# A two-layer transformer on one core: the batch-1 projection becomes steps of the attention program

## The reference

```python
x = layernorm(x + L0_attn(x))   # 16 heads of 16, causal softmax
x = layernorm(x + L0_ffn(x))    # silu(x Wu') * (x Wg') Wd', weights ternary
x = layernorm(x + L1_attn(x))   # 16 query heads, 4 key/value heads, ALiBi,
                                # a window and the global columns masked out
x = layernorm(x + L1_ffn(x))    # silu gate, width 1024

def ternary_quant(w):
    scale = mean(|w|) + 1e-8
    return clip(round(w / scale), -1, 1) * scale
# layer 1 only: queries come from x * sigmoid(sum |x|), keys and values from x
```

## Time and the profile before

| | |
|---|---|
| median of 3 runs | 1161.24 us |
| profiled execution, its own time | 1158.14 us |
| its span | 1156.4 us |
| layer 0: projection, from first transposes to last part | 6.9 to 73.7 us |
| layer 0: opening maxima | 74.6 to 101.0 us |
| layer 0: first exponential's scores | 104.8 us |
| layer 1: projection | 495.1 to 539.2 us |
| layer 1: opening maxima on DVE | 553.4 to 589.5 us |
| layer 1: first exponential's scores | 593.2 us |
| mean granted clock of PE, share of full speed | 0.939 |

### The profile page before, as it was taken

One profiled execution on the slowest core, in us unless ns is written; L12 is line 12 of the kernel. 1 busy time (PEld: TensorE's weight loads), 2 busy tenths in 40 slices (PEclk: granted clock), 3 DMA queues, 4 the chain that ended last, 5 costly groups with the idle time before them and its releaser, 6 DMA issues. The chain is left out here.

```text
span 1156.4 us, 17918 instructions
## 1 busy us (share of the span) xinstructions
PE 1022.1 (88%) x6546; PEld 516.8 (45%) x6546; DVE 725.0 (63%) x1563; ACT 591.5 (51%) x1169; POOL 324.2 (28%) x391
## 2 busy tenths in 40 slices
PE   7947899999988899765779899999999999899996
PEld 4511233333324788642122334334343334588885
DVE  3767877777744655464878677777778744234322
ACT  3412666666675433234026577776777776523220
POOL 1041111111112343302225614224152341324331
PEclk9955999999999999978569899999999999999998
DMA  8585044443000000007932416143260000000001
GB/s 276 127 155 70 1 56 56 56 56 50 7 2 1 2 1 1 1 19 163 235 103 73 103 16 118 36 82 90 29 118 4 32 2 1 1 1 19 19 1 37
DMA packets 32980, 64.20 MB, mean 56 GB/s; under 512 B 6079, under 2 KB 22351, under 8 KB 30516
## 3 DMA queue, kind: packets, MB, share of 16 engines
q1 hardware_dynamic: 31004, 58.07, 25.3%
q0 software_dynamic: 1072, 3.80, 0.9%
q10 hardware_dynamic: 816, 1.18, 0.3%
HBM read 50.45 MB, written 12.32 MB: 54 GB/s over the span
## 5 line engine op out<-in xcount | busy, mean ns | idle before, releaser
L812 ACT ACTIVATE prob<-ps 128x512 f32<-128x512 f32 (+6 forms) x896 | 442.9, 537 | 293.9 <-PE ps L848 286.2
L848 PE MATMUL ps<-qop,kop 98*128 98x512 bf16 (+15 forms) x1376 | 303.5, 292 | 21.1 <-ACT prob L812 8.0
L834 PE MATMUL ps<-kop,qop 96*128 96x512 bf16 (+3 forms) x896 | 273.7, 381 | 53.0 <-DVE maxes L753 24.4
L848 PEld LDWEIGHTS ps<-qop,kop 107*128 107x128 bf16 (+2 forms) x1376 | 114.6, 98 | 280.1 <-ACT prob L812 201.1
L875 PE MATMUL ps<-prob,vst 128*32 128x512 f32 (+4 forms) x1792 | 212.3, 546 | 6.8 <-POOL prob L702 4.7
L753 DVE CUSTOM_DVE_ANT_0 attn<-ps,alibi_table 128x960 bf16<-128x960 f32 x128 | 148.1, 1157 | 87.8 <-PE ps L834 59.0
L702 POOL TENSOR_TENSOR prob<-prob,keep 128x384 int32<-128x384 int32 (+2 forms) x144 | 122.3, 852 | 268.7 <-ACT prob L812 266.5
L1229 PE MATMUL ps<-xs,ffn_parts 128*128 128x512 f32 x640 | 150.4, 392 | 4.5 <-DVE hf L1203 2.3
L753 DVE CUSTOM_DVE_ANT_0 tri<-ps,alibi_table 128x960 bf16<-128x960 f32 x128 | 147.6, 1153 | 3.5 <-PE ps L834 3.5
L834 PEld LDWEIGHTS ps<-kop,qop 96*128 96x128 bf16 x896 | 77.7, 100 | 143.6 <-DVE maxes L753 84.1
L1229 PEld LDWEIGHTS ps<-xs,ffn_parts 128*128 128x128 f32 x640 | 119.0, 188 | 29.7 <-DVE hf L1203 3.1
(11 more groups left out here) (97 smaller groups left out, 710.0 us busy)
## 6 DMA issues: line engine op xcount, KB each, us to landing
alibi_table<-in_table SPq DMA_DIRECT2D x32, 464.0 KB, 5.7
qop<-q_parts SPq DMA_DIRECT2D x96, 128.0 KB, 7.1
kop<-k_parts SPq DMA_DIRECT2D x48, 128.0 KB, 7.7
kop<-k_parts SPq DMA_DIRECT2D x48, 96.0 KB
q_parts<-qop SPq DMA_DIRECT2D x8, 384.0 KB, 3.0
q_parts<-kop SPq DMA_DIRECT2D x8, 384.0 KB, 6.5
x<-in_x SPq DMA_DIRECT2D x4, 512.0 KB, 7.3
out<-x SPq DMA_DIRECT2D x4, 512.0 KB, 2.9
```

The lines of the kernel that those rows point to most:

```text
L812: nc.scalar.activation(prob[0:rows, q % 2, k % HG, lo % CH:lo % CH + hi - lo], ps[0:rows, t_bank(n, k), lo % CH:lo % CH + hi - lo], ACT.Ex ...
L834: last = nc.tensor.matmul(ps[:, S_BANK + 2 * (k % S_SLOTS) + a // CH, a % CH:a % CH + b - a], qop[0:RD, par, h, i0:i0 + P], kop[0:RD, par, ...
L848: return nc.tensor.matmul(ps[0:rows, bank, a % CH:a % CH + b - a], lhs, rhs, start=start, stop=True, skip_group_check=True)
```

## The change

The program `project` is gone; a class `Projection` gives its work as steps of the attention program, so there is one barrier less in each layer.

- The opening is now: all steps of batch 0, then the 32 maxima of group 0 with the steps of batch 1 spread among the first 30 of them, in layer 0 then the three sums of absolutes and the thresholds.
- Turns, units and value items share three PSUM banks (4, 5, 6) in place of six; banks 0 to 3 serve the maxima.
- In batch 0 the copies of turns are shared by ACT and DVE; in batch 1 ACT makes them all, and POOL makes the third parts.
- Layer 0's units run in the order q, k of the first two groups (four units), then of the other two. After four units are stored, SP loads group 0.
- The operand rows are interleaved: product row r of feature d is partition 6d + r instead of 16r + d, so each transfer writes every sixth partition.
- Layer 1 weighs, exponentiates and scales x chunk by chunk instead of all at once, with two chunk buffers.
- The sums of absolute weights move to ACT (one activation with an accumulator for each of three tensors, 128x2048). The ternary weights move to POOL, as twelve steps in groups 1 to 3 of layer 0, each of two comparisons and one subtraction over 128x512. The raw weights are loaded after group 0's operands.
- Layer 1's six table loads are issued first. POOL adds the bias behind the opening instead of beside it.

```diff
+        if layer.index == 0 and 1 <= group <= 3 and selected(layer, half, kt) is None:
+            steps.append(("ternary", 4 * (group - 1) + kt, 0))
...
+def opening_of(layer, proj):
...
+    first = proj.steps(0)
+    behind = proj.steps(1) + [("flush", 0)]
+    maxima = [("max", u, 1) for u in range(len(units_of(layer)))]
+    end = []
+    if layer.index == 0:
+        behind += [("abs", j) for j in range(3)]
+        end = [("total", 0, 0), ("threshold", 0, 0)]
+    out = [(what, k, 0) for what, k in first]
+    for n, unit in enumerate(maxima):
+        out.append(unit)
+        upto = [-(-len(behind) * m // (len(maxima) - 2)) for m in (n, n + 1)]
+        out += [(what, k, 0) for what, k in behind[upto[0]:upto[1]]]
+    return out + end + [("parts", 0, 1), ("rows", 0, 1)]
...
+    BANKS, SIDE = (4, 5, 6), 7
...
+            self.units = [(b, m, c) for b in range(B) for p in range(KD) for c in range(2) for m in (p, KD + p)]
...
+    def steps(self, b):
+
+        half, turned = len(self.units) // 2, len(self.turns) // 2
+        units = [("unit", u) for u in range(b * half, (b + 1) * half)]
+        turns = [("turn", n) for n in range(b * turned, (b + 1) * turned)]
+        if self.i == 0:
+            vs = [("v", v) for v in range(b * 4, b * 4 + 4)]
+            first = [o for j in range(4) for o in (*units[2 * j:2 * j + 2], vs[j])]
+            return turns + first
+        if b == 1:
+            return turns + units + [("v", 1)]
+        out = []
+        for c in range(2):
+            out += [("weigh", c), *turns[4 * c:4 * c + 2], ("divide", c), ("scale", c), *turns[4 * c + 2:4 * c + 4]]
+        out += [*units[:3], ("weigh", 2), *units[3:5], ("weigh", 3), units[5], ("v", 0)]
+        return out + [(what, c) for c in (2, 3) for what in ("divide", "scale")]
...
+    def third_part_behind(self, pool, u):
...
+        self.nc.gpsimd.tensor_tensor(self.part[u % RING][0:r, 2, :], self.rest[0:r, u % RING, :],
+                                     self.part[u % RING][0:r, 1, :], ALU.subtract).then_inc(self.part3[1], 1)
...
+            nc.scalar.activation(self.below, self.raw[k], ACT.Abs, accum_out=self.wsum[:, k:k + 1]
+                                 ).then_inc(self.abs_sum, 1)
...
+            j, cols = k // 4, slice(k % 4 * CH, (k % 4 + 1) * CH)
+            pool.wait_ge(self.tern, 3 + 3 * k)
+            for which, side in enumerate((self.above, self.below)):
+                nc.gpsimd.tensor_scalar(side[:, cols], self.raw[j][:, cols], self.thr[:, which, j:j + 1], 0.0,
+                                        (ALU.is_gt, ALU.is_lt)[which], ALU.add).then_inc(self.tern, 1)
+            pool.wait_ge(self.tern, 5 + 3 * k)
+            nc.gpsimd.tensor_tensor(self.K.wffn[:, j, 0, cols], self.above[:, cols].bitcast(F32),
+                                    self.below[:, cols].bitcast(F32), ALU.subtract).then_inc(self.tern, 1)
...
-            rows = slice(HD * r, HD * (r + 1))
+            rows = slice(r, NPAIR * HD, NPAIR)
...
+            operands.constants(sp, 0)
+            operands.constants(sp, 1)
+
+            for u in range(4):
+                proj.send(sp, u)
+            proj.wait_sent(sp, 4)
+            operands.load(sp, 0)
+            later = len(proj.units) // 2 + 2 + 2 * (1 - i)
+            for u in range(4, later):
+                proj.send(sp, u)
             operands.load(sp, 1)
-            for k in range(RING):
-
-                sp.wait_ge(operands.sent[k], K.parts_in_dram[k])
+            for u in range(later, len(proj.units)):
+                proj.send(sp, u)
+            send_rows(0)
+            proj.wait_sent(sp, len(proj.units))
             operands.constants(sp, BUFS - 1)
             operands.load(sp, BUFS - 1)
```

More of the change, by code:

```diff
@@ L594, in attend @@
         v_heads = HG if i == 0 else 1
+        maxes = sb(st, "maxes" + tag, [P, HG, TB], F32)
+        sums = [sb(st, f"sums{n}" + tag, [P, T], BF16)[:] if n == 0 or i == 0 else K.tri[:] for n in range(2)]
         vst = sb(st, "vst" + tag, [P, BUFS, TB + i, v_heads, 2 * HD], F32)
@@ L605, in attend @@
         rec = sb(st, "rec" + tag, [P, 2, CT * HG], F32)
-        opening = [("max", u, 1) for u in range(NU)] + [("parts", 0, 1), ("rows", 0, 1)]
+        proj = Projection(nc, sem, sb, st, K, L, dram, prep, prob, K.before_weights)
+        opening = opening_of(L, proj)
         def exp_slots(n):
@@ L719, in step @@
                         prep.inverse(pool, k, 0)
+                    elif what in Projection.STEPS:
+                        proj.pool(pool, what, k)
             zero = nc.gpsimd.to_reg(0.0) if i == 0 else None
+            if i == 0:
+                pool.wait_ge(loaded[0], 16 * operands.loads)
+                for j, wt in enumerate(dram.ffn[0]):
+                    wt = wt.rearrange("(k p) n -> p k n", p=P)
+                    pool.dma_start(proj.raw[j].rearrange("p (k n) -> p k n", k=wt.shape[1]), wt
+                                   ).then_inc(proj.ffn_loaded, 16)
+            step(-1, opening)
+            pool.wait_ge(proj.v_done, (8, 1)[i])
             stage(0, 0)
+            pool.wait_ge(proj.xt_full, len(proj.turns))
+            pool.wait_ge(K.tri_loaded, 16 * 5)
             for t in range(NT):
@@ L791, in step @@
                         ).then_inc(normed, 1)
+                    elif what in Projection.STEPS:
+                        proj.dve(dve, what, k)
                     elif what in Preparation.STEPS:
@@ L821, in step @@
                         nc.scalar.copy(ot[:], ps[:, O_BANK, :]).then_inc(evicted, 1)
+                    elif what in Projection.STEPS:
+                        proj.act(act, what, k)
                     elif what in Preparation.STEPS:
                         prep.act(act, what, k)
+            if i == 0:
+                act.dma_start(proj.w[:], dram.wq[0].rearrange("(k p) n -> p k n", p=P)).then_inc(proj.w_loaded, 16)
+            else:
+                act.dma_start(proj.w[:, :, 0:D], dram.wq[1].rearrange("(k p) n -> p k n", p=P)
+                              ).then_inc(proj.w_loaded, 16)
+                act.dma_start(proj.w[:, :, D:proj.width], dram.wkv.rearrange("(k p) n -> p k n", p=P)
+                              ).then_inc(proj.w_loaded, 16)
+            step(-1, opening)
             all_groups(step)
@@ L904, in step @@
                     elif what == "exp":
+                        if n == 0 and k == 0:
+                            proj.wait_all_read(pe)
                         if k == 0:
```

560 lines of the change are left out of this document (285 added, 275 removed).

## The result

The changed kernel takes 1168.65 us (median of 6 runs, 1165.53 to 1172.36) against 1160.77 for the kernel before in the same comparison (6 runs): a ratio of 1.0068, interval 1.0047 to 1.0089. The change made the kernel slower by 0.7%, where 1126 us had been forecast. The profiled execution took 1167.41 us, with a span of 1165.7 and a mean granted clock of 0.942.

What follows compares the result with a forecast made beforehand. Each layer's border was taken as a serial chain: project both batches, load, maxima, exponentials. Gains of 25 us (layer 0) and 10 (layer 1), with 0 behind the borders, took the span from 1156.4 to 1121, median 1126; range 1113 to 1146.

Steps and rivals of the forecast that it cites:

- the ternary step: Layer 0, groups 1 to 3 on GpSimd: 2.3 to 3.9 us a step, four hidden in a 14.99 us gap; taken as 0.
- from 3.7 us a ternary step on, each group's fourth mask is late: Rival, GpSimd late in layer 0's groups: 1141 us at 5 a step, 1174 at 7.7; chance 0.06.
- The residual adds: GpSimd's 10.92 us of adds, now after layer 1's last third part: up to 5 us without the load's cover, taken as 0.
- the third ahead of nothing urgent: Later operand loads on SP (groups 1, 2), issued behind more waits: needed some 30 us later, no cost counted.
- Turns start at 6.9, so units start near 10.6: Start of layer 0: only batch 0's four turns stand ahead of the first unit, which starts near 10.6 us.
- I take issue plus 2 us: 8 us for either layer: First operand load with interleaved rows, each layer: 8 us, bounds 6 (issue alone) and 14.6 (old).
- the load stays slow: Rival: the operand load's shape costs what it cost, both first scores come 6 us later: 1138 us; chance 0.15.
- The tail of layer 0's opening: From the end of layer 0's maxima (76) to the first exponential (79.7): 3.7 us, as before.
- Layer 0's opening: 32 maxima with batch 1 among them: 40 us, PE the bound, bounds 34 and 51; layer 0's gain 25 us.
- Layer 1: Units 12.5 us behind first turn, first score 36.6, opening 46.5 with DVE the bound, exponentials 88; gain 10 us.
- the slower rival: Both openings stay at 1.2 GHz with PE the bound, 67.6 and 64 us: 1171 us; chance 0.05.
- The series of the two works: Upper bounds of the openings, maxima and batch 1 one after the other: 51 us in layer 0, 58 in layer 1.

Runs made afterwards that it cites:

- 21.6 in the experiment: Changed kernel with its twelve ternary steps spread two to a gap over groups 1 to 6 instead of four in groups 1 to 3: 1146.17 us, ratio 0.9882.
- 9.3 together by the experiment's times: Changed kernel with GpSimd's residual adds moved under the opening, eight after the first operand load, eight after the last turn: 1158.68 us, ratio 0.9988.
- 7.7 by the experiment: Changed kernel with layer 1's first feed-forward weight load issued on SP ahead of group 2's operand load: 1159.5 us, ratio 1.0002.
- the mended version: Changed kernel with ternary steps two per gap, adds under the opening, gate weights first, constants behind x, and layer 0's sum and thresholds behind the row transpose: 1124.55 us.
- the experiment gave 14.1 and 9.0: Kernel of 1124.55 us with all of batch 1's projection steps put ahead of the first maximum in both openings: 1146.4 us, ratio 0.9879.
- The four single edits: Changed kernel with one edit each: two ternary steps per gap 1146.17 us, adds under the opening 1158.68, gate weights first 1159.5, constants behind x 1161.09.

## Why the prediction was wrong

**The step that failed is the ternary step, costed at nothing.** "no row has a compare, so from the 128x1024 cast at 1.03, halved, 0.5, up to the subtraction's 1.29" was a bound from rows of another operation, and the comparison took 2.00 us, above both. The step was to be 2.3 to 3.9 us and is 5.44; "Hidden, or 0.5 us over, three times" became 7.8 us, three times (23.5 in the intervals, 21.6 in the experiment). The prediction had its threshold right. Its rival "from 3.7 us a ternary step on, each group's fourth mask is late", with a chance of 0.06, gives, at 5.44, 4 x 1.74 = 7.0 us a group. That this is near the 7.8 is partly luck: PE waited 5.2 us for the mask, and the fall of its clock behind that wait, which the prediction did not count, brought the rest. The error was to treat the highest row at hand as the top of the range for an operation that no row showed, with the threshold of harm (3.7) inside that range. With two steps in a gap (15.0 us there, from the first comparison at 137.91 to the mask at 152.91) any price up to 7.5 would have been harmless.

**The other terms that were mis-sized:**

- *The residual adds: "Without that cover they cost up to 5 us; I take 0."* The cast was 6.4 us longer for them in layer 1; by the marks they cost 5.2 us there and 1.4 in layer 0, and 9.3 together by the experiment's times. And not where the prediction looked (a late mask): a short cast on DVE did not finish until POOL's adds did. The Trainium skill (SBUF — State Buffer, Who interferes with whom) says that copies, casts and operations with a scalar on DVE can take a port pair that they share with GpSimd, whoever comes second being blocked. The rows agree: cast 6.58 us beside the adds, 0.18 without. That it is these ports, and not something else of POOL's adds, no run shows by itself. The prediction did not use the rule.
- *"the third ahead of nothing urgent".* It was ahead of layer 1's first weight load, which is issued 9 us later for it, and through POOL's cut and the mask behind it that reached PE: 6.3 us in group 0, 7.7 by the experiment. The prediction counted what the moved load needs, not what its thirteen issues of 0.6 us stand in front of.
- *"Turns start at 6.9, so units start near 10.6."* Constants that were loaded behind x before are now issued beside it: turns in two pieces, first unit at 14.69. With the constants behind x it was 10.87.
- *"I take issue plus 2 us: 8 us for either layer."* The load took 9.7. The two microseconds behind the last issue were right (42.55 less 40.4); the issue was not, 0.63 us each in place of 0.47. The rival "the load stays slow" did not happen: with contiguous rows it was 15.2.
- *The tail of layer 0's opening: "3.7 us later, as before".* 6.2: the thresholds and the sum over partitions stand in it, slowed by the same adds (1.02 us for two operations that take 0.24 without them).

**What was right.** Layer 0's opening: 40 forecast, 39.75 measured, PE the bound. Layer 1: units 12.5 us behind the first turn (11.8), first score 36.6 behind it (36.1), opening 46.5 (43.3), exponentials 88 (89.6, with the long cast in them; 85.2 in the mended version). The granted clock rose in both openings from 0.50 to 0.89, with PE busy for 90% of the time in layer 0 and 80% in layer 1; the slower rival, a clock that stays at 1.2 GHz, did not happen, though the kernel became slower. The series of the two works was bounded at 11 us more than the overlap in layer 0 and 11.5 in layer 1; the experiment gave 14.1 and 9.0.

**One part of the result is probably not the change's.** In the stretch from the last row transpose of layer 0 to layer 1's first turn, the changed kernel took 165.2 us and the kernel before 161.1, over the same steps. Windows of ten microseconds from the end of the attention on, in the kernel before, in the changed one, and in the kernel before with interleaved rows:

```profile
374.01:384.01 10.00, 7.26 (x47) 5.85 (x48) 5.05 (x11) 4.73 (x7) 0.88 (x1) 1.00 0.01 3
```

```profile
381.39:391.39 10.00, 7.42 (x30) 5.45 (x31) 3.23 (x8) 3.73 (x5) 0.00 (x0) 0.57 0.01 2
```

```profile
369.50:379.50 10.00, 7.27 (x32) 5.50 (x33) 3.61 (x9) 3.54 (x5) 0.00 (x0) 0.66 0.01 2
```

PE's steps there are the same, with pauses that differ by under 0.2 us, and the clock fell to 1.2 GHz in two and not in the first. It fell in all twelve other profiles, and in the kernel before with interleaved rows the stretch is 163.9 us. So some 3 us of the profiled difference look like a fall of the clock that this one execution of the kernel before was spared, and not like the change. That fits its own time, 1158.14, under a median of 1160.77, and the spans differ by 9.3 where the medians differ by 7.9. The later executions of the kernel before fit too: those at a mean clock of 0.939 or 0.940 took 1157.9 to 1159.45 us, those at 0.934 to 0.936 took 1160.49 to 1162.84. In which stretch their clock fell, no trace shows.

**The account.** By the medians the changed kernel is 42.7 us above the forecast. The four single edits give back, by the ratios, 21.6 + 9.3 + 7.7 + 6.0 = 44.6, and the version with all of them takes 1124.55, close to the 1126 forecast. Its marks stand against the forecast ones as follows: first exponential of layer 0 at 81.0 (79.7), from there to layer 1's first turn 392.3 us (390.4 forecast, the stretch of before, without the clock's fall), from first turn to first exponential 85.2 (88), the rest 563.3 (563.2). So the nearness holds in each part to 3 us, and the parts' errors of +1.3, +1.9 and -2.8 cancel, which is luck. It shows that the chain the prediction described is there, and that what hid it were four positions in queues that the prediction had costed at nothing or passed over.

## What to carry to other kernels

When steps are moved, walk each in-order queue behind the place where they arrive and ask what stands there, not only what the moved step itself needs: here an engine with 15 us of idle time cost 22 us because four steps went into one gap, and the same work spread over more gaps cost nothing. A wait that is put into PE's work costs more than its length where the clock falls with it: here 5.2 us of waiting became 6.9 to 8.5. An operation that no row shows has no upper bound from rows of other operations; if the argument turns at a value near that bound, place it so that a price twice as high is still harmless. An overlap is worth at most the time of the second engine, so filling the first engine's remaining waits may give nothing once the second one binds.

## What the runs showed of the hardware that I had not expected

- GpSimd's comparison of 128x512 float32 with one scalar for each partition takes 2.00 us with a second operation and 1.57 without; its subtraction of two tensors of that size takes 1.27, and DVE does the comparison in 0.48.
- A DVE cast of 128x32 was held up for 6.4 us by GpSimd's adds, more than nine of them in a row (0.68 us each): it did not get in between two of them. In layer 0 the same cast beside the same adds took 0.78 us; why so much less is open. DVE's maxima, which read PSUM and tables, ran beside the same adds at their usual 1.15 us.
- A load whose transfers write every sixth partition is issued more slowly on SP (0.63 us each against 0.46) and moves its bytes faster: 9.7 us from first issue to first score in place of 15.2.
- Five small loads issued at the start beside 2 MB of x made PE's first unit start 3.8 us later.
- Waits of 5.2 us in PE's otherwise dense work each brought its clock down to 1.2 GHz for 7 to 10 us; the next matmuls of that group took 1.94 us for eight in place of 1.07.
